# Choosing the expert on VectorE, from a spread rank, instead of closing the others on TensorE

## The reference

```python
x = x + attention(layernorm(x))
h = layernorm(x).reshape(-1, 128)
logits = h @ gate_w.T
top_v, sel = max(logits), argmax(logits)      # the first maximum wins
rw = sigmoid(top_v)
for e in range(8):
    mask = (sel == e)
    xs = h * (rw * mask)[:, None]
    out = out + (xs @ w_up[e].T) * silu(xs @ w_gate[e].T) @ w_down[e].T
return x + out
```

## Time and profile before

| | |
|---|---|
| median of 3 runs | 566.31 us (564.96 to 567.15) |
| the profiled execution | 562.29 us, its span 560.6 us |
| PE busy | 533.4 us, 95% |
| DVE busy | 449.8 us, 80% |
| ACT busy | 385.0 us, 69% |
| POOL busy | 211.2 us, 38% |

### The profile page before, as it was taken

One profiled execution on the slowest core, in us unless ns is written; L12 is line 12 of the kernel. 1 busy time (PEld: TensorE's weight loads), 2 busy tenths in 40 slices (PEclk: granted clock), 3 DMA queues, 4 the chain that ended last, 5 costly groups with the idle time before them and its releaser, 6 DMA issues.

```text
span 560.6 us, 12273 instructions
## 1 busy us (share of the span) xinstructions
PE 533.4 (95%) x4674; PEld 234.5 (42%) x4674; DVE 449.8 (80%) x668; ACT 385.0 (69%) x771; POOL 211.2 (38%) x393
## 2 busy tenths in 40 slices
PE   8559899999999999999999999999988999999996
PEld 6324434333343333433434334334223555666553
DVE  6938899999999999999999999999924655655631
ACT  7224688898998998988989899899886322222221
POOL 5577264443363444533544346314142111111100
PEclk9769999999999999999999999999999999999999
DMA  6151122320211511102232021120030112121000
GB/s 174 30 168 52 37 64 73 111 66 10 65 37 36 168 28 57 56 18 69 80 104 68 10 66 42 43 69 10 7 100 4 48 56 62 56 58 57 19 20 19
DMA packets 27866, 32.45 MB, mean 58 GB/s; under 512 B 4384, under 2 KB 21280, under 8 KB 27808
## 3 DMA queue, kind: packets, MB, share of 16 engines
q1 hardware_dynamic: 27664, 31.28, 19.2%
q10 hardware_dynamic: 144, 0.39, 0.2%
HBM read 20.26 MB, written 11.01 MB: 56 GB/s over the span
## 4 chain that ended last, share of the span: by engine, by line
PE 70%; DVE 18%; ACT 4%; POOL 3%; issue 2%; DMA 2%; ACTq 1%; POOLq 0%; DVEq 0%
PE ps L1062 19%; PE ps L1046 13%; PE ps L1003 8%; DVE top_p L825 7%; DVE top_p L827 6%; PE ps L1115 6%; PE ps L1123 5%; PE ps L1112 5%; ACT prob L681 4%; DVE top_p L820 3%; PE ps L1013 3%; PE ps L947 2%; PE ps L938 2%; PE ps L1113 2%; PE ps L1021 1%
## 5 line engine op out<-in xcount | busy, mean ns | idle before, releaser
L681 ACT ACTIVATE prob<-ps 128x512 f32<-128x512 f32 (+2 forms) x640 | 307.5, 560 | 41.6 <-PE ps L1046 36.8
L827 DVE TENSOR_REDUCE top_p<-ps 128x2 f32<-128x1024 f32 x192 | 223.6, 1217 | 5.4 <-PE ps L1013 1.8
L1046 PE MATMUL ps<-q_rows,k_rows 51*128 51x512 bf16 (+3 forms) x768 | 168.9, 328 | 2.7 <-ACT prob L681 1.4
L1062 PE MATMUL ps<-prob,v_all 128*9 128x512 f32 (+3 forms) x1536 | 156.8, 488 | 0.7 <-ACT sum_sb L672 0.4
L581 POOL TENSOR_SCALAR_AFFINE_SELECT prob<-prob 128x512 f32<-128x512 f32 x128 | 81.4, 636 | 184.8 <-ACT prob L681 183.0
L1003 PE MATMUL ps<-k_rows,q_rows 48*128 48x512 bf16 (+2 forms) x896 | 130.7, 305 | 8.9 <-DMA k_rows<-split_parts 6.9
L1046 PEld LDWEIGHTS ps<-q_rows,k_rows 51*128 51x128 bf16 x768 | 52.4, 93 | 135.4 <-ACT prob L681 120.0
L825 DVE TENSOR_REDUCE top_p<-ps 128x4 f32<-128x1024 f32 x64 | 76.4, 1214 | 3.5 <-PE ps L1013 3.3
L1003 PEld LDWEIGHTS ps<-k_rows,q_rows 48*128 48x128 bf16 x896 | 42.8, 94 | 45.3 <-issue 15.5
L724 ACT ACTIVATE prob<-ps 128x512 f32<-128x512 f32 x32 | 19.1, 597 | 56.0 <-PE ps L1113 56.0
L903 DVE TENSOR_TENSOR prob<-ps,prob 128x512 f32<-128x512 f32 x32 | 22.1, 690 | 36.9 <-PE ps L1115 36.9
(11 more groups left out here) (90 smaller groups left out, 430.1 us busy)
## 6 DMA issues: line engine op xcount, KB each, us to landing
split_parts<-part SPq DMA_DIRECT2D x6, 768.0 KB, 5.1
q_rows<-split_parts SPq DMA_DIRECT2D x31, 96.0 KB
k_rows<-split_parts SPq DMA_DIRECT2D x31, 96.0 KB
value_sums<-sum_sb SPq DMA_DIRECT2D x128, 18.0 KB
x_sb<-x SPq DMA_DIRECT2D x8, 256.0 KB, 4.5
qk<-value_sums SPq DMA_DIRECT2D x8, 256.0 KB, 3.6
qk<-inverse_sums SPq DMA_DIRECT2D x8, 256.0 KB, 3.8
out<-y SPq DMA_DIRECT2D x8, 256.0 KB, 2.3
```

The lines of the kernel that those rows point to most:

```text
L681: a.activation(prob[:, i % NB, g0:g0 + heads, 0:cols], ps[:, load_at(u, n) % 3, 0:heads * cols].rearrange("p (s t) -> p s t", s=heads), AC ...
L827: return v.tensor_reduce(top_p[:, place, qt, s:s + 3:2], banks, AX.X, ALU.max)
L1046: last = mm(ps[:, l % 3, m * cols:(m + 1) * cols], k_rows[rows, k, s + m, j * P:(j + 1) * P], q_rows[rows, k, s + m, c * HALF + q0:(c + 1) ...
L1062: last = mm(ps[32 * g:32 * g + HD + 1, BANK_V, q0:HALF], v_all[:, b, j, first_head + g, :], prob[:, i % NB, g, 0:n], start=(j == 0), stop= ...
```

## The change

The closing products go, and with them shut, refused, its turning and its copy. Instead the rank (the maximum of hit times ramp: 8 for the first expert, 1 for the last) is spread: PE multiplies it, as a stationary tile that is the same in all 128 columns, with the identity, so that every row of a bank holds the ranks of all tokens (spread_rank), and ACT copies this to rank_b. DVE then does for each pair choose: Silu = (rank_b == rank of the row's expert) * Silu, one instruction over 128 x 512, and back waits for it. rank_of holds each row's expert rank and is set by eight small memsets on DVE. The spread uses the bank of the even gates.

The rows' weighting moves from DVE to ACT: weigh_rows does tanh, the scaling by 0.5 plus 0.5, and the four tiles of xs, each with a wait for the one before except among the four. It stands where tanh stood, between Silu 1 and Silu 2.

PE's order in a step becomes: gate 0, gate 1, turn_xn, up 0, gate 2, logits, up 1, gate 3, up 2, up 3, project3, spread_rank, turn_xs, down. Before step 1, spread_rank and turn_xs now stand behind the wait for the last sums. At startup POOL no longer builds shut.

```diff
-        shut = sb("shut", [EXPERTS, EXPERTS * INNER], BF16)
+        rank_of = sb("rank_of", [P, PAIRS])
...
-        first = sb("first", [P, 2, TPH])
-        refused = sb("refused", [P, 2, TPH, EXPERTS], BF16)
-        refused_t = sb("refused_t", [EXPERTS, HALF], BF16)
+        rank = sb("rank", [P, 2, TPH], BF16)
+        rank_b = sb("rank_b", [P, 2, HALF])
...
+        BANK_RANK = BANK_GATE[0]
@@ gpsimd, startup
-            last.then_inc(const_set, 1)
-            chain.link(g.memset(shut[:], MASKED))
-            chain.link(g.affine_select(out=shut[:], ...))
-            g.affine_select(out=shut[:], ...).then_inc(const_set, 1)
+            last.then_inc(const_set, 2)
@@ scalar
-            def tanh(n, h):
+            def weigh_rows(n, h):
                 act.wait_ge(best_set, n)
-                a.activation(weight[:, h, :], best[:, h, :], ACT.Tanh, scale=0.5).then_inc(tanh_set, 1)
-
-            def copy_refused(n):
-                act.wait_ge(refused_turned, n)
-                a.activation(refused_t[:], ps[0:EXPERTS, BANK_ROUTE, :].bitcast(BF16)[:, HALF:],
-                             ACT.Copy).then_inc(refused_t_set, 1)
+                a.activation(weight[:, h, :], best[:, h, :], ACT.Tanh, scale=0.5).then_inc(act_chain, 1)
+                act.wait_ge(act_chain, 2 * n - 1)
+                a.activation(weight[:, h, :], weight[:, h, :], ACT.Copy, scale=0.5, bias=0.5).then_inc(act_chain, 1)
+                act.wait_ge(act_chain, 2 * n)
+                for i in range(TPH):
+                    last = a.activation(xs[:, h, i, :], xn[:, h, i, :], ACT.Copy, scale=weight[:, h, i:i + 1])
+                last.then_inc(xs_set, 1)
+
+            def copy_rank(n, h):
+                act.wait_ge(rank_mm, n)
+                hold(act, hidden_set, 4 * (n - 2))
+                a.activation(rank_b[:, h, :], ps[:, BANK_RANK, :], ACT.Copy).then_inc(rank_b_set, 1)
@@ vector
+            for e in range(EXPERTS):
+                last = v.memset(rank_of[INNER * (e % 2):INNER * (e % 2 + 1), e // 2:e // 2 + 1], float(EXPERTS - e))
+            last.then_inc(rank_of_set, 1)
...
-                chain.link(v.tensor_reduce(first[:, h, :], hit[:, h], AX.X, ALU.max))
-                v.tensor_tensor(refused[:, h], hit[:, h],
-                                first[:, h, :, None].to_broadcast((P, TPH, EXPERTS)),
-                                ALU.not_equal).then_inc(refused_set, 1)
-                dve.wait_ge(tanh_set, n)
-                chain.link(v.tensor_scalar(weight[:, h, :], weight[:, h, :], 0.5, 0.5, ALU.mult, ALU.add))
-                for i in range(TPH):
-                    last = v.tensor_scalar(xs[:, h, i, :], xn[:, h, i, :], weight[:, h, i:i + 1], None, ALU.mult)
-                last.then_inc(xs_set, 1)
+                v.tensor_reduce(rank[:, h, :], hit[:, h], AX.X, ALU.max).then_inc(rank_set, 1)
+
+            def choose(n, h, pr):
+                n_pr = 4 * (n - 1) + pr + 1
+                dve.wait_ge(rank_b_set, n)
+                dve.wait_ge(silu_set, n_pr)
+                v.scalar_tensor_tensor(silu[:, pr % 2, :], rank_b[:, h, :], rank_of[:, pr:pr + 1],
+                                       silu[:, pr % 2, :], ALU.is_equal, ALU.mult).then_inc(chosen_set, 1)
 
             def back(n4, pr):
                 dve.wait_ge(up_mm, n4 + pr + 1)
-                dve.wait_ge(silu_set, n4 + pr + 1)
+                dve.wait_ge(chosen_set, n4 + pr + 1)
...
+                choose(n, h, 0)
                 back(n4, 0)
+                choose(n, h, 1)
                 back(n4, 1)
                 if n < STEPS:
                     route(n + 1, 1 - h)
-                back(n4, 2)
-                back(n4, 3)
+                for pr in (2, 3):
+                    choose(n, h, pr)
+                    back(n4, pr)
@@ tensor
-            def turn_refused(n, h):
...
+            def spread_rank(n, h):
+                pe.wait_ge(rank_set, n)
+                hold(pe, silu_set, 4 * (n - 1) - 1)
+                for i in range(TPH):
+                    last = mm(ps[:, BANK_RANK, i * P:(i + 1) * P], rank[:, h, i:i + 1].to_broadcast((P, P)),
+                              ident_b[:], start=True, stop=True)
+                last.then_inc(rank_mm, 1)
...
-                gate = ps[:, BANK_GATE[pr % 2], :]
-                mm(gate, w_g[:, cols], xs_t[:, h, :], start=True, stop=False)
-                mm(gate, shut[:, cols], refused_t[:], start=False, stop=True).then_inc(gate_mm, 1)
+                mm(ps[:, BANK_GATE[pr % 2], :], w_g[:, pr * P:(pr + 1) * P], xs_t[:, h, :], start=True, stop=True
+                   ).then_inc(gate_mm, 1)
...
-            turn_refused(1, 0)
-            turn_xs(1, 0)
             pe.wait_ge(exp_done, load_at(UNITS, 0))
             pe.wait_ge(sum_set, 2 * UNITS)
+            spread_rank(1, 0)
+            turn_xs(1, 0)
...
-                back(n, n4, h, 0)
+                gate(n, n4, h, 0)
+                gate(n, n4, h, 1)
                 if more:
                     turn_xn(n + 1, 1 - h)
-                back(n, n4, h, 1)
+                up(n4, h, 0)
+                gate(n, n4, h, 2)
                 if more:
                     logits(n + 1, 1 - h)
-                back(n, n4, h, 2)
-                back(n, n4, h, 3)
+                up(n4, h, 1)
+                gate(n, n4, h, 3)
+                up(n4, h, 2)
+                up(n4, h, 3)
                 if n + 2 <= STEPS:
                     project3(n + 2, h)
                 if more:
-                    turn_refused(n + 1, 1 - h)
+                    spread_rank(n + 1, 1 - h)
                     turn_xs(n + 1, 1 - h)
                 down(n, n4)
```

More of the change, by code:

```diff
@@ L270, in layer_kernel @@
         best_set = sem("best_set")
[L271 to L274, removed]
+        act_chain = sem("act_chain")
+        rank_of_set = sem("rank_of_set")
+        rank_set = sem("rank_set")
+        rank_mm = sem("rank_mm")
+        rank_b_set = sem("rank_b_set")
         xs_set = sem("xs_set")
@@ L280, in layer_kernel @@
         silu_set = sem("silu_set")
+        chosen_set = sem("chosen_set")
         hidden_set = sem("hidden_set")
@@ L715, in lead_in @@
                 if i == FRONT[2] + 1:
-                    tanh(1, 0)
+                    weigh_rows(1, 0)
             step(UNITS - 1, lead_in)
@@ L724, in back @@
                 a.activation(silu[:, pr % 2, :], ps[:, BANK_GATE[pr % 2], :], ACT.Silu).then_inc(silu_set, 1)
-            copy_refused(1)
+            copy_rank(1, 0)
             copy_xs(1, 0)
@@ L735, in _ @@
                 if more:
-                    tanh(n + 1, 1 - h)
+                    weigh_rows(n + 1, 1 - h)
                 back(n4, 2)
@@ L739, in _ @@
                 if more:
-                    copy_refused(n + 1)
+                    copy_rank(n + 1, 1 - h)
                     copy_xs(n + 1, 1 - h)
@@ L914, in _ @@
             residual(2, 0, 1)
+            dve.wait_ge(rank_of_set, 1)
             for n in range(1, STEPS + 1):
@@ L1092, in logits @@
                 last.then_inc(logit_mm, 1)
-            def turn_refused(n, h):
-                pe.wait_ge(refused_set, n)
-                turned_rows = ps[0:EXPERTS, BANK_ROUTE, :].bitcast(BF16)[:, HALF:]
+            def spread_rank(n, h):
+                pe.wait_ge(rank_set, n)
+                hold(pe, silu_set, 4 * (n - 1) - 1)
                 for i in range(TPH):
-                    last = nc.tensor.transpose(turned_rows[:, i * P:(i + 1) * P], refused[:, h, i, :], ident_b[:])
-                last.then_inc(refused_turned, 1)
+                    last = mm(ps[:, BANK_RANK, i * P:(i + 1) * P], rank[:, h, i:i + 1].to_broadcast((P, P)),
+                              ident_b[:], start=True, stop=True)
+                last.then_inc(rank_mm, 1)
             def turn_xs(n, h):
@@ L1103, in turn_xs, with gate, up @@
                 turn_tiles(xs[:, h], BANK_TURN).then_inc(xs_turned, 1)
-            def back(n, n4, h, pr):
+            def gate(n, n4, h, pr):
                 if pr == 0:
+                    pe.wait_ge(rank_b_set, n)
                     pe.wait_ge(xs_t_set, n)
-                    pe.wait_ge(refused_t_set, n)
-                cols = slice(pr * P, (pr + 1) * P)
                 hold(pe, silu_set, n4 + pr - 1)
-                gate = ps[:, BANK_GATE[pr % 2], :]
-                mm(gate, w_g[:, cols], xs_t[:, h, :], start=True, stop=False)
-                mm(gate, shut[:, cols], refused_t[:], start=False, stop=True).then_inc(gate_mm, 1)
+                mm(ps[:, BANK_GATE[pr % 2], :], w_g[:, pr * P:(pr + 1) * P], xs_t[:, h, :], start=True, stop=True
+                   ).then_inc(gate_mm, 1)
+            def up(n4, h, pr):
                 hold(pe, hidden_set, n4 + pr - 1)
-                mm(ps[:, BANK_UP[pr % 2], :], w_u[:, cols], xs_t[:, h, :], start=True, stop=True
+                mm(ps[:, BANK_UP[pr % 2], :], w_u[:, pr * P:(pr + 1) * P], xs_t[:, h, :], start=True, stop=True
                    ).then_inc(up_mm, 1)
```

## The result

The changed kernel took 574.55 us (median of 4 runs, 569.33 to 577.61), the kernel before 566.73: a ratio of 1.0151, interval 1.011 to 1.0192. Forecast were +4.1 us and a range up to 575.0, and 574.55 lies just inside it. A second set gave 574.24 against 565.51, a ratio of 1.0167 (1.0127 to 1.0208). The medians and ratios of this and all later sets leave out executions in a slower state (581.59 us of the changed kernel, and 933.22 of one of its variants). The profiled execution is 574.18 us, 11.9 above that of before, which was one of the kernel's quicker ones (562.29).

A forecast was written before the change was run, and what follows sets the result against it. PE's instruction list bounded a step, until ACT's and DVE's longer path delayed the down products. Terms -0.8 + 2.3 + 1.4 + 1.1 + 1.0 - 0.85 = +4.15 us gave a median of 570.4 us, 8-in-10 range 566.2 to 575.0.

The forecast's parts named there:

- the sum: Whole kernel: startup, end of attention and steps 1 to 8 added to +4.15 us against the profiled 562.29.
- the end of the attention: Lead-in to step 1: weigh_rows delays exponentials +1.65, spread and turn_xs wait +0.65; together +2.3 us, bounds +1.6 and +3.2.
- the startup: Before the first stores: POOL no longer building shut frees DVE's L786 and neighbours; -0.8 us, bounds -0.3 and -1.1.
- The path from up 1 to the down products: In a step, hidden 1, route, ACT's tiles, Silu, choose and hidden delay the down products: 7.26 us from up 1.
- the collisions: DVE's choose, with two SBUF inputs, held up by POOL's weigh; the sum expected this in step 3 alone, about 0.8 us.
- PE's slots: PE's times within a step: 0.96 us per gate or up product, 0.44 per turn, 0.79 for the logits.
- Step 3: choose meets POOL's weigh, starting 8.88 us after gate 0, and waits: +1.1 us, bounds +0.2 and +1.5.
- Step 7: Has no projection, but its down products wait for the same hidden 3: 15.91 against 14.88 us, +1.0.
- Step 8: Has no route; DVE's own queue ends it, down products at 9.03 us against 9.88: -0.85.
- ACT's tiles were not cheap: First rival: ACT's tiles at 0.19 us each and choose at 0.66, giving 566.5 us, no change; chance 0.18.
- PE did not keep setting the end: Second rival: up 1 to down products under 5.79 us, so PE's saving comes through, 559.1 us; chance 0.09.
- the third rival: choose and POOL's weigh collide in every step, up to 1.26 us in steps 1, 2, 4, 5, 6: 575.4 us; chance 0.13.

The follow-up runs named there:

- the fill run: Changed kernel plus 18 idle PE turns of 128 columns in the pause before the down products of steps 1 to 7: 569.37 us, ratio 1.0066.
- the run with the old order: Changed kernel with weigh_rows behind Silu 3 and PE's order as before (gate, up, gate, up): 554.43 us, ratio 0.9832.

## Why the prediction was wrong

The step that failed is the sum's silence on PE's clock. The prediction put a new pause in front of seven bursts of down products and priced it at its length alone; it named "a granted clock under 1.00 in the steps, now that PE pauses" only among what would prove it wrong, and gave it neither a term nor a chance. The falls in the steps were worth 4.9 us by the fill run, about 5.7 with what the idle turns cost.

The mechanism of the pause was right: Silu 2 behind weigh_rows, then choose, hidden and the down products. But three terms that were in the sum were mis-sized as well, which the time alone does not show:

- For gate 0 of step 1 to the down products of step 8 the sum had 1.4 + 1.1 + 1.0 - 0.85 = +2.65; measured without the lower clock were +0.3.
- For the end of the attention it had +2.3; at a fall of equal length the change cost 0.8.
- For the startup it had -0.8; measured were -0.4.

Together they are some +0.7 us (0.3 + 0.8 - 0.4) where +4.15 was forecast, an estimate from single profiles. The other 11 us between the two profiles are 4.9 and 1.5 in the steps, 3.6 at the end of the attention and 1.1 in front of it, all in stretches where the changed kernel's profile has the lower clock at times and that of before has not. Executions at an equal mean clock say about the same: at 0.979 the fill kernel took 565.16 us and before 564.60 and 565.79, at 0.973 it took 568.39 to 569.18 and before 566.89 and 567.03, with 0.85 us of idle turns in the former. So that the fill run's +3.9 lies beside the forecast's +4.15 is luck, and so, in part, is the right direction: without the clock the change would have been close to even. Term by term:

- **The path from up 1 to the down products** was counted as 7.26 us and measured 7.36 (461.52 to 468.88). In it the tiles on ACT came 0.30 us apart (463.96 to 465.15 for four), with 0.29 taken; ACT waiting for itself cost 0.02 to 0.04, not 0.1; choose took 0.75, not 0.72 (its mean of 785 ns has the collisions). The Trainium skill, "ScalarE: Activation LUTs", section What ACT_TABLE_LOAD costs, gives 186 ns plus 0.833 ns a column, 93 ns for each value read per partition, and 93 ns of overlap; as an estimate that is 0.39 us for such a tile and 0.29 from one to the next, and the trace agrees (four in 1.28, 0.30 apart).
- **PE's slots**: a gate or up product takes 0.86 us beside its like; the 0.96 of the earlier trace rows was that of a float32 product next to the closing one. So up 1 began at 4.68, not 5.07, the down products at 12.04, not 12.33, and a step was 15.72, not 15.91. It also means that PE's own list is at most 13.9 us, by the run with the old order: leaving the closing products out frees 1.7 us a step, not 1.2.
- **Step 3** was to be 1.1 longer than before and was 0.3 (15.95 against 15.67): weigh began 8.15 us after gate 0 and not 8.88, choose 2 lost 0.24 us to it, and project3's wait for weigh fell into the pause.
- **Step 7** keeps the pause without having the projection, as said: 17.34 with the lower clock, or 15.7 without. **Step 8** took 8.76 to the down products; 9.03 was forecast.
- **Startup** gave 0.4, not 0.8. DVE's own stretch became 0.8 shorter; what took the other half back was not traced.
- **End of the attention**: the exponentials waited 1.66 us behind the start of tanh, against 0.11 before: +1.55, with +1.65 forecast. With PE at the lower clock meanwhile, only 0.8 of it and of the +0.65 behind the last sums is left in the time to gate 0.
- **The rivals.** ACT's tiles were not cheap. PE did not keep setting the end. The collisions exist, but they met a choose in two steps only, once covered and once for 0.24 us; one per step, as in the third rival, did not come.

What stays open is how far the longer waits at the end of the attention lengthen its stretch at the lower clock, and why only about every second of equal pauses is followed by a fall.

## What to carry to other kernels

Before moving work to an idle engine, ask what stands behind it in that engine's queue. Six cheap instructions on an engine that was busy for 28% of a step cost 16.8 us more there than two places later, because a ready Silu had to wait behind a wait for another engine. Moving a product ahead on PE moves another behind, and its reader may have something urgent queued behind it. And where PE has been busy without a break, price a new pause twice: its length, and a chance that the work behind it runs at half clock. If the pause can't be removed, idle turns in it are worth trying.

## What the runs showed that was not expected

- Behind a pause of 2.0 to 2.2 us in front of the down products, PE's granted clock fell to a half in about every second case (3 and 4 of the six such pauses in the changed kernel's two profiles, 3 of 6 in the kernel before with a pause, 2 of 2 with the weighting on DVE, 1 of 1 with the old order), and behind one of 3.07 us as well; each fall cost 1.63 us. Behind shorter ones in the same place (0.2 to 1.8 us, in all the kernels that have them) it fell in none. With idle turns in the pause it did not fall either.
- The kernel before, whose steps have no pauses, also loses clock in some executions, at the end of the attention: 562.14 us at a mean clock of 0.987, 567.75 at 0.970.
- Two lines of one engine's order were worth 16.8 us (574.24 to 557.43), about twice the whole slowdown of 8.7.
